# Two attentions: the first unit's loads between the stores, dummy products on PE, and other orders

## The chip, the cores and the metric

The kernel is one program on one core of a Trainium2 chip (trn2). Its time is the device time of the whole program in microseconds, as the median of several runs. PE is the engine of matrix products (TensorE), with PEld for its weight loads; DVE, ACT and POOL are the vector, scalar and general-purpose engines; SP issues transfers. All of them work through their own list of instructions in order and wait for each other by semaphores.

## The reference, cut to what matters

The program is eight layers on 2 x 1024 tokens of width 256. The change touches the first and the seventh, causal attentions with grouped heads: 32 query and 8 key heads of width 8, and 16 query and 4 key heads of width 16. Both are, cut:

```python
q = rope(x @ Wq); k = rope(x @ Wk); v = x @ Wv      # 4 query heads share a key head
att = where(causal, q @ k.T / sqrt(hd), -inf)        # 1024 x 1024 for each head
y = softmax(att) @ v
x = x + y @ Wo + b
```

## The kernel before, in words

`Attention` (one class for both widths, `hd`) works in units: one key head of one batch with its four query heads, 1024 positions. Width 8 has 16 units, width 16 has 8. Positions are cut in blocks of 128.

**Preparation.** For each of four groups of 512 tokens, PE makes the projections, DVE rotates them, PE transposes them, and ACT writes each as three bf16 parts (`part1` to `part3`, L952; PE takes the parts off with `less1` and `less2`, L1039). SP stores the parts to DRAM, twelve stores, n = 0 to 11 (L699), from a ring of five buffers; ACT waits until the buffer of store n - 5 is free. Stores 0 to 5 are the first batch's.

**Loads.** `load_copy` brings a unit's queries and keys back in the layout for the products, six transfers of queries (L667) and three of keys (L668). Width 8 loads each unit twice, to partitions 0 and 64 (`copies`), so that two products can run in both halves of PE; `max_at` is 64 there, and 0 in width 16, which has one copy.

**A unit.** First come the row maxima, in 22 pieces k (`MAX_STEPS`): PE makes scores without them (`max_scores`, L1116), DVE reduces them (L877). POOL splits the maxima into bf16 parts (L778 to L785), PE transposes them (`turn_max`, L1135; the first unit does it in two halves, `turn_first_max`, L1126), DVE copies them out (L895, L886), and SP puts them as three rows under the unit's queries (`load_max`, L685; `load_first_max`, L679). With these rows the 36 score steps (`scores`, L1162) give scores less their maximum; ACT exponentiates (L996), POOL masks the diagonal (L807), and twelve value products (`values`, four heads each, L1178) sum into one bank. ACT copies the sum (L988), PE transposes it (`turn_out`, L1143), DVE normalizes (L907, L910).

**Order.** All engines follow the tables in `ORDERS`. The maxima of a unit stand between the score steps of the unit before it, or of the one before that: `max_at` gives the step for each k, negative ones in the unit two ahead. `turn_max`, `turn_out1`, `turn_out0` give the steps of the transpositions, `values_at` those of the value products, `own_at` (first unit alone) those of its own second half of maxima. Products of maxima and the transpositions go through a ring of two bank pairs: each waits until DVE has emptied the item two before it. A unit's first max_scores (k = 0) waits for its loads:

```python
if k == 0:
    pe.wait_ge(self.q_in1.sem, self.q_in1.at((u + 1) * (16 * len(self.terms))))
...
if self.max_at and k == (HALF1 if u == 0 else 0):
    pe.wait_ge(self.q_in0.sem, self.q_in0.at((u + 1) * (16 * len(self.terms))))
```

`warm` (L127) issues products of 512 columns whose result nobody reads.

## Time and profile before

| | |
|---|---|
| median of 3 runs | 1870.91 us (1862.11 to 1872.44) |
| the profiled execution | 1867.24 us, its span 1865.5 us |
| busy in the span | PE 1723.6, DVE 1125.2, ACT 800.0, POOL 539.3 us |
| width 8: preparation, units | 20 to 59.5 us, 59.5 to 490 us |
| width 16: preparation, units | 1369 to 1412 us, 1412 to 1658 us |

Busy time over the whole span says little, since the layers have different limits; the windows and the waits of a stretch tell which engine the others stand behind. The granted clock is that of PE, as a share of its upper level of 2.4 GHz; 0.50 is its lower level, 1.2 GHz.

### The profile page before, as it was taken

The page shows a single profiled execution, that of the slowest core. Times are in us where ns is not written, and L with a number is a line of the kernel's source. Part 1 is how long each engine was busy: PE and PEld are TensorE (multiplying, and loading weights), DVE is VectorE, ACT ScalarE, POOL GpSimd, SP SyncE. Part 2 cuts the span into 40 slices and gives each one's busy share as a digit, 9 for nine tenths or more (in the row PEclk, how much of TensorE's full clock was granted, in tenths as well). Part 3 has the DMA queues.
Part 4 walks back from the last instruction along what each step waited for, and adds up shares of the span by engine and source line. Part 5 has one row for each costly group of instructions (what it writes and reads, how often), then busy time and mean ns, then how long its engine had stood idle before and what let it go on. Part 6 is the DMA issues. An engine that isn't in the chain of part 4 may idle for free.

```text
span 1865.5 us, 32053 instructions
## 1 busy us (share of the span) xinstructions
PE 1723.6 (92%) x10972; PEld 1038.9 (56%) x10972; DVE 1125.2 (60%) x3171; ACT 800.0 (43%) x1469; POOL 539.3 (29%) x852
## 2 busy tenths in 40 slices
PE   7689999999999999898999989999986999999997
PEld 4122222222579998466999946667552333355774
DVE  6689999998442221875222265834566988836444
ACT  3368888888533331113233211222132677752221
POOL 2412222222211111551121140257324122221770
PEclk9689999999999999989999999999986999999999
DMA  3322222221310000301000050123513222001334
GB/s 113 86 59 69 68 67 66 61 63 45 100 61 24 29 24 25 97 1 57 24 27 27 21 192 8 53 74 102 155 49 79 44 44 41 6 2 59 96 102 147
DMA packets 86045, 115.03 MB, mean 62 GB/s; under 512 B 20186, under 2 KB 63874, under 8 KB 85634
## 3 DMA queue, kind: packets, MB, share of 16 engines
q1 hardware_dynamic: 74753, 82.58, 15.9%
q0 software_dynamic: 11136, 30.42, 5.1%
q8 instruction: 92, 1.51, 0.3%
q14 instruction: 64, 0.52, 0.1%
HBM read 78.30 MB, written 33.69 MB: 60 GB/s over the span
## 4 chain that ended last, share of the span: by engine, by line
PE 64%; DVE 22%; DMA 5%; issue 2%; ACT 1%; POOL 1%; SPq 1%; DVEq 0%; ACTq 0%; POOLq 0%
PE psum L1665 15%; DVE region_a L877 15%; PE psum L1677 7%; PE psum L1178 6%; PE psum L1909 5%; PE psum L1162 5%; PE psum L1116 4%; PE psum L1880 4%; PE psum L1891 2%; DMA y_norm<-region_a 2%; PE psum L1928 2%; PE psum L1929 2%; PE psum L437 2%; PE psum L1018 1%; PE psum L2356 1%
## 5 line engine op out<-in xcount | busy, mean ns | idle before, releaser
L877 DVE CUSTOM_DVE_ANT_0 region_a<-psum,region_a 128x128 bf16<-128x128 f32 (+7 forms) x768 | 533.3, 754 | 64.9 <-PE psum L1116 61.7
L996 ACT ACTIVATE region_w<-psum 128x512 f32<-128x512 f32 x864 | 463.2, 601 | 166.7 <-PE psum L1162 152.2
L1178 PE MATMUL psum<-region_w,region_a 128*32 128x512 f32 (+3 forms) x2304 | 245.3, 504 | 2.4 <-issue 0.6
L1764 DVE TENSOR_TENSOR region_a<-psum,region_a 128x512 f32<-128x512 f32 x76 | 52.5, 691 | 297.3 <-PE psum L1665 297.3
L807 POOL TENSOR_SCALAR_AFFINE_SELECT region_w<-region_w 128x512 f32<-128x512 f32 x192 | 121.9, 635 | 370.7 <-ACT region_w L996 297.5
L1116 PE MATMUL psum<-region_a,y_norm 48*128 48x512 bf16 (+7 forms) x816 | 184.7, 356 | 22.9 <-DVE region_a L877 20.4
L1162 PE MATMUL psum<-y_norm,region_a 51*128 51x512 bf16 (+1 forms) x612 | 180.9, 396 | 12.8 <-DMA y_norm<-region_a 10.7
L1546 POOL DMA_INDIRECT region_a<-token_rows,region_a x116 | 113.6, 980 | 161.8 <-DVE region_a L1522 81.9
L1665 PE MATMUL psum<-region_a,ctx 128*128 128x128 f32 x1280 | 148.0, 277 | 1.1 <-DVE region_a L1739 1.1
L1665 PEld LDWEIGHTS psum<-region_a,ctx 128*128 128x128 f32 x1280 | 147.5, 194 | 2.5 <-DVE region_a L1739 1.6
L1162 PEld LDWEIGHTS psum<-y_norm,region_a 51*128 51x128 bf16 (+1 forms) x612 | 46.5, 96 | 172.1 <-ACT region_w L996 121.7
L1677 PE MATMUL psum<-region_w,region_a 128*128 x608 | 137.7, 380 | 1.4 <-ACT region_a L1701 1.4
L1665 PE MATMUL psum<-region_a,y_norm 128*128 128x128 f32 x1152 | 131.7, 275 | 1.8 <-DVE region_a L1739 1.8
L1665 PEld LDWEIGHTS psum<-region_a,y_norm 128*128 128x128 f32 x1152 | 131.3, 192 | 3.1 <-DVE region_a L1739 2.3
L1550 POOL DMA_INDIRECT answer_rows<-region_a x38 | 37.5, 987 | 322.7 <-ACT region_a L1701 322.7
L1677 PEld LDWEIGHTS psum<-region_w,region_a 128*128 128x128 f32 x608 | 112.6, 190 | 15.9 <-issue 2.2
L1116 PEld LDWEIGHTS psum<-region_a,y_norm 48*128 48x128 bf16 (+1 forms) x816 | 52.2, 98 | 102.4 <-DVE region_a L877 71.9
L1909 PE MATMUL psum<-region_w,region_a 128*128 x312 | 108.1, 470 | 0.5 <-issue 0.4
L1178 PEld LDWEIGHTS psum<-region_w,region_a 128*32 128x32 f32 x2304 | 47.8, 108 | 91.2 <-issue 47.9
L1701 ACT ACTIVATE region_a<-psum 128x256 f32<-128x256 f32 x38 | 14.6, 383 | 182.7 <-PE psum L1677 182.7
L1722 ACT ACTIVATE region_a<-psum 128x512 f32<-128x512 f32 x76 | 44.8, 589 | 103.6 <-PE psum L1665 103.6
L1880 PE MATMUL psum<-y_t,region_w 128*128 128x512 f32 (+1 forms) x192 | 86.1, 596 | 0.9 <-ACT ctx L1995 0.9
(226 smaller groups left out, 2539.1 us busy)
## 6 DMA issues: line engine op xcount, KB each, us to landing
y_norm<-a_q SPq DMA_DIRECT2D x132, 64.0 KB
token_rows<-y_norm SPq DMA_DIRECT2D x16, 512.0 KB, 4.7
y_norm<-answer_rows SPq DMA_DIRECT2D x16, 512.0 KB, 6.1
y_norm<-b_q SPq DMA_DIRECT2D x36, 128.0 KB
region_w<-in_f_wg SPq DMA_DIRECT2D x8, 512.0 KB, 4.4
region_w<-in_f_wu SPq DMA_DIRECT2D x8, 512.0 KB, 4.3
region_w<-in_f_wd SPq DMA_DIRECT2D x1, 4096.0 KB, 14.5
region_w<-answer_rows SPq DMA_DIRECT2D x8, 512.0 KB, 8.5
```

Source lines behind the costliest of these rows:

```text
L807: pool.affine_select(p, p, pattern=[[0, GQ], [1, P]], channel_multiplier=-1, base=0, compare_op=ALU.is_ge, fill=0.0)\
L877: last = dve.tensor_tensor_reduce(self.masked_scores[place % 2][:, at:at + n], both[:, at:at + n], self.causal[:, SEQ - n:SEQ], scale=-1.0 ...
L996: act.activation(self.p[col % P_RING][:, :, i % 4, :], c.bank[ST_BANKS[s % 3]].rearrange("p (h t) -> p h t", h=GQ), ACT.Exp, scale=self.sc ...
L1116: mm = pe.matmul(c.bank[bank + b][:, to:to + cols], qp[rows, h, P * i:P * i + P], kp[rows, lo:lo + cols], start=True, stop=True, skip_grou ...
L1162: mm = pe.matmul(bank[:, :], self.kp[slot][rows, P * j:P * j + P], self.qp[slot][rows, :, P * i:P * i + P], start=True, stop=True)
L1178: mm = pe.matmul(c.bank[ACC_BANK][32 * h:32 * h + 32, P * lo:512], self.vp[slot][:, j, :], self.p[col % P_RING][:, h, lo:4, :], start=(j = ...
L1546: pool.indirect_dma_start(y, None, self.c.tokens[:, :], bass.IndirectOffsetOnAxis(ap=self.row_in[:, k:k + 1], axis=0)).then_inc(done.sem, 16)
L1665: mm = pe.matmul(bank[:, P * q:P * q + P], w[:, f, 512 * half + P * q:512 * half + P * q + P], self.yt[:, f, :], start=(f == 0), stop=(f = ...
L1677: mm = pe.matmul(c.bank[7][:, 0:D], self.h[k % 2][:, j, :], self.wd[:, bass.ds((own * (last + 1) + j) * D, D)], start=(j == 0), stop=(j == ...
L1764: dve.tensor_tensor(h[:, at], c.bank[2 + half][:, :], self.g[:, at], ALU.mult)\
L1880: mm = pe.matmul(c.bank[6 * (n % 2) + k][0:m, :], weight[:, f, P * j:P * j + m], c.yt[:, f, 512 * g:512 * g + 512], start=(f == 0), stop=( ...
L1909: mm = pe.matmul(self.gu_bank[j][:, 0:2 * self.hidden], self.yt[j][:, f, :], w.wgu[:, f, bass.ds(owner[k] * (2 * self.hidden), 2 * self.hi ...
```

## The change

Three things change in both attentions. The nine loads of unit 0's copy are cut into three parts (`load_part`) and stand between stores 6 to 8 (the second copy of width 8 between 9 to 11), where they stood in one piece behind store 5 (and 8); on SP, unit 1's copy at partition 0 moves behind the first half of unit 0's rows. PE gets dummy products: 10 in the last group of the preparation, 33 between unit 0's first ten maxima, two in each of its first six steps. The tables of `ORDERS` get other numbers: both of width 8, and the first unit's of width 16. The diff:

```diff
--- before.py
+++ after.py
@@ -75,17 +75,17 @@
         return [k for k, at in enumerate(self.own_at, len(MAX_STEPS) - len(self.own_at)) if at == s]
 
 
-VALUES_8 = [8, 13, 16, 18, 20, 24, 26, 32, 35, 38, 41, 42]
+VALUES_8 = [6, 9, 19, 19, 21, 23, 28, 30, 33, 36, 38, 39]
 VALUES_16 = [6, 9, 12, 17, 22, 28, 31, 35, 35, 38, 41, 41]
 ORDERS = {
-    8: (FirstOrder([0, 0, 0, 0, 0, 0, 0, 0, 1, 1, 1, 2], 6, 9,
-                   [5, 6, 9, 9, 9, 9, 12, 14, 14, 14, 14, 16, 16, 18, 19, 20, 20, 21, 21, 24, 24, 26],
-                   30, 10, 34, VALUES_8, 6, 17, 28),
-        Order([-11, -10, -9, -4, -4, -1, 1, 2, 3, 5, 6, 8, 8, 9, 11, 13, 14, 17, 18, 20, 21, 22],
-              30, 10, 29, VALUES_8, 6, 17, 24)),
-    16: (FirstOrder([0, 1, 2, 2, 2, 2, 3, 4, 5, 5, 6, 7], 8, 9,
-                    [8, 8, 9, 9, 9, 10, 12, 13, 13, 14, 16, 16, 17, 18, 18, 20, 20, 20, 22, 22, 24, 28],
-                    32, 33, 23, VALUES_16, 5, 19, 28),
+    8: (FirstOrder([1, 2, 2, 2, 2, 2, 2, 2, 2, 3, 3, 3], 5, 9,
+                   [0, 1, 3, 3, 6, 7, 9, 9, 9, 9, 9, 9, 10, 12, 12, 12, 14, 16, 18, 20, 21, 22],
+                   28, 15, 26, VALUES_8, 3, 18, 24),
+        Order([-12, -9, -6, -6, -4, -3, -1, 1, 2, 3, 5, 6, 7, 9, 10, 12, 14, 16, 19, 20, 21, 22],
+              28, 15, 26, VALUES_8, 3, 18, 25)),
+    16: (FirstOrder([0, 1, 2, 2, 3, 3, 3, 4, 4, 5, 5, 6], 7, 9,
+                    [7, 8, 8, 9, 9, 9, 10, 11, 12, 12, 12, 12, 13, 13, 13, 15, 16, 18, 21, 22, 23, 23],
+                    33, 33, 33, VALUES_16, 5, 19, 27),
          Order([-9, -8, -7, -5, -2, -1, 0, 0, 3, 4, 6, 6, 8, 8, 10, 12, 13, 14, 17, 19, 21, 23],
                33, 33, 25, VALUES_16, 5, 19, 29)),
 }
@@ -656,18 +656,20 @@
                          (self.bias_out, d["bias_out"].partition_broadcast(P)),
                          (self.mq, d["mq"])):
             sp.dma_start(dst, src).then_inc(self.wo_in.sem, 16)
+        def load_part(u, slot, at, a):
+
+            q_in, k_in = (self.q_in1, self.k_in1) if at == self.max_at else (self.q_in0, self.k_in0)
+            row = at + hd * sum(1 for term in self.terms if term[0] < a)
+            n = sum(1 for term in self.terms if term[0] == a)
+            q = self.q_dram[a, bass.ds(u * (GQ * hd), GQ * hd), :].rearrange("(h d) t -> d h t", d=hd)
+            for m in range(n):
+                sp.dma_start(self.qp[slot][row + hd * m:row + hd * m + hd, :, :], q).then_inc(q_in.sem, 16)
+            sp.dma_start(self.kp[slot][row:row + hd * n, :], self.k_dram[0:n, bass.ds(u * hd, hd), :])\
+                .then_inc(k_in.sem, 16)
+
         def load_copy(u, slot, at):
-
-            q_in, k_in = (self.q_in1, self.k_in1) if at == self.max_at else (self.q_in0, self.k_in0)
-            row = at
             for a in range(3):
-                n = sum(1 for term in self.terms if term[0] == a)
-                q = self.q_dram[a, bass.ds(u * (GQ * hd), GQ * hd), :].rearrange("(h d) t -> d h t", d=hd)
-                for m in range(n):
-                    sp.dma_start(self.qp[slot][row + hd * m:row + hd * m + hd, :, :], q).then_inc(q_in.sem, 16)
-                sp.dma_start(self.kp[slot][row:row + hd * n, :], self.k_dram[0:n, bass.ds(u * hd, hd), :])\
-                    .then_inc(k_in.sem, 16)
-                row += hd * n
+                load_part(u, slot, at, a)
 
         def load(u, slot):
             for at in reversed(self.copies):
@@ -698,17 +700,19 @@
             sp.wait_ge(self.part3.sem, self.part3.at(n + 1))
             sp.dma_start(dst.rearrange("a f t -> f a t"), self.parts[n % PARTS][0:rows, :, :])\
                 .then_inc(self.parts_out[n % PARTS].sem, 16)
-            if n == 3 * NG // NB - 1:
-                self.parts_stored(sp, n + 1)
+            later = n - 3 * NG // NB
+            if later == 0:
+                self.parts_stored(sp, n)
                 sp.wait_ge(self.pads.sem, self.pads.at(self.slot_pads * 2))
-                load_copy(0, 0, self.max_at)
-            if n == 3 * NG // NB + 2 and self.max_at:
-                load_copy(0, 0, 0)
+            if 0 <= later < 3 * len(self.copies):
+                load_part(0, 0, self.copies[-1 - later // 3], later % 3)
         for q_in, k_in in ((self.q_in0, self.k_in0), (self.q_in1, self.k_in1))[0 if self.max_at else 1:]:
             sp.wait_ge(q_in.sem, q_in.at(16 * len(self.terms)))
             sp.wait_ge(k_in.sem, k_in.at(48))
-        load(1, 1)
+        load_copy(1, 1, self.max_at)
         load_first_max(0)
+        for at in self.copies[:-1]:
+            load_copy(1, 1, at)
         self.parts_stored(sp, 3 * NG)
         sp.wait_ge(self.pads.sem, self.pads.at(self.slot_pads * SLOTS))
 
@@ -1050,6 +1054,11 @@
             for q in range(4):
                 if g < NG:
                     multiply(4 * g + q)
+                elif q == 1:
+                    pe.wait_ge(self.v_done.sem, self.v_done.at(NT))
+                    c.warm(pe, 3, 2)
+                elif q:
+                    c.warm(pe, 3, 3)
                 if g > 1 and q == 0:
                     less2(n - 1)
                 if g and q == 0:
@@ -1064,9 +1073,9 @@
                 if g and q == 3:
                     less1(n + 2)
                     less2(n + 1)
+        c.warm(pe, 3, 2)
         less2(3 * NG - 1)
 
-        pe.wait_ge(self.v_done.sem, self.v_done.at(NT))
         pe.wait_ge(self.rotm.sem, self.rotm.at(3 * NT if hd == 8 else NT + 1))
         pe.wait_ge(self.wo_in.sem, self.wo_in.at(16 * 3))
 
@@ -1195,6 +1204,8 @@
                 if left > 1:
                     for k in self.order.early_maxima(s):
                         max_scores(u + 2, k, (slot + 2) % SLOTS)
+                if first and s < order.values_at[0]:
+                    c.warm(pe, ACC_BANK, 2)
                 if left and s == order.turn_max:
                     turn_max(u + 1)
                 if not first and s == order.turn_out1:
@@ -1209,10 +1220,16 @@
 
         for k in range(HALF1):
             max_scores(0, k, 0)
+            if k == 1:
+                pe.wait_ge(self.part3.sem, self.part3.at(3 * NG))
+            if k:
+                c.warm(pe, ACC_BANK, 2)
+        c.warm(pe, ACC_BANK, 5)
         turn_first_max(0)
         for k in range(HALF1, HALF1 + 4):
             max_scores(0, k, 0)
-        pe.wait_ge(self.part3.sem, self.part3.at(3 * NG))
+            c.warm(pe, ACC_BANK, 3)
+        c.warm(pe, ACC_BANK, 6)
         self.each_unit(unit)
         for col, at in enumerate(self.order.values_at):
             if at >= len(STEPS):
```

The first place is SP's queue behind store 5, at the end of the preparation of width 8 (stores are a_q and a_k as targets, loads have them as sources). Before:

```order
L699 DMA a_k<-region_a 64x3x512
L667 DMA y_norm<-a_q 8x4x1024 x3
L668 DMA region_a<-a_k 24x1x1024
L667 DMA y_norm<-a_q 8x4x1024 x2
L668 DMA region_a<-a_k 16x1x1024
L667 DMA y_norm<-a_q 8x4x1024
L668 DMA region_a<-a_k 8x1024
L699 DMA a_q<-region_a 128x3x512 x2
L699 DMA a_k<-ctx 64x3x512
L667 DMA y_norm<-a_q 8x4x1024 x3
```

With the change:

```order
L701 DMA a_k<-region_a 64x3x512
L701 DMA a_q<-region_a 128x3x512
L666 DMA y_norm<-a_q 8x4x1024 x3
L667 DMA region_a<-a_k 24x1x1024
L701 DMA a_q<-region_a 128x3x512
L666 DMA y_norm<-a_q 8x4x1024 x2
L667 DMA region_a<-a_k 16x1x1024
L701 DMA a_k<-ctx 64x3x512
L666 DMA y_norm<-a_q 8x4x1024
L667 DMA region_a<-a_k 8x1024
L701 DMA a_q<-ctx 128x3x512
L666 DMA y_norm<-a_q 8x4x1024 x3
```

Stores 6, 7 and 8 each stand ahead of a part of the loads, and no longer behind all nine.

The second place is PE at unit 0's first score step of width 8 (the product whose inputs wait for the rows, m_in0), with the semaphores that each waits for. Before:

```order
L1162 MATMUL psum<-y_norm,region_a 128x512 [waits attn_k_in0,attn_m_in0,attn_q_in0,attn_part3]
L1116 MATMUL psum<-region_a,y_norm 128x512 [waits attn_ring_done]
L1116 MATMUL psum<-region_a,y_norm 128x256
L1116 MATMUL psum<-region_a,y_norm 128x512 [waits attn_ring_done]
L1116 MATMUL psum<-region_a,y_norm 128x256
```

With the change:

```order
L127 MATMUL psum<-identb 128x512 x9
L1171 MATMUL psum<-y_norm,region_a 128x512 [waits attn_m_in0,attn_k_in0,attn_q_in0]
L1125 MATMUL psum<-region_a,y_norm 128x128 [waits attn_q_in0,attn_ring_done,attn_k_in0,attn_k_in1,attn_q_in1]
L1125 MATMUL psum<-region_a,y_norm 128x128 x3
L127 MATMUL psum<-identb 128x512 x2
L1171 MATMUL psum<-y_norm,region_a 128x512
L1125 MATMUL psum<-region_a,y_norm 128x512 [waits attn_ring_done]
L1125 MATMUL psum<-region_a,y_norm 128x256
```

Behind the first score product now stands k0 of unit 1 (four products of 128 columns), which waits for both copies of unit 1; before, unit 0's own maxima k10 and k11 stood there.

The third place is PE in a steady unit of width 8 around the transposition of the next unit's maxima (L1135 before, L1144 with the change), from step 27 on. Before:

```order
L1116 MATMUL psum<-region_a,y_norm 128x384 x2
L1162 MATMUL psum<-y_norm,region_a 128x512 x2
L1143 MATMUL psum<-identf,region_a 128x128 x4
L1162 MATMUL psum<-y_norm,region_a 128x512
L1135 MATMUL psum<-identb,region_a 96x128
L1162 MATMUL psum<-y_norm,region_a 128x512 x2
L1116 MATMUL psum<-region_a,y_norm 128x384 x2
L1116 MATMUL psum<-region_a,y_norm 128x512 x2
L1178 MATMUL psum<-region_w,region_a 32x512 x4
L1162 MATMUL psum<-y_norm,region_a 128x512 x3
L1116 MATMUL psum<-region_a,y_norm 128x512 x2
L1178 MATMUL psum<-region_w,region_a 32x512 x4
```

With the change, from step 27 too:

```order
L1171 MATMUL psum<-y_norm,region_a 128x512
L1125 MATMUL psum<-region_a,y_norm 128x256 x4
L1171 MATMUL psum<-y_norm,region_a 128x512
L1144 MATMUL psum<-identb,region_a 96x128
L1187 MATMUL psum<-region_w,region_a 32x512 x4
L1171 MATMUL psum<-y_norm,region_a 128x512 x2
L1125 MATMUL psum<-region_a,y_norm 128x384 x4
L1187 MATMUL psum<-region_w,region_a 32x512 x4
L1171 MATMUL psum<-y_norm,region_a 128x512 x2
L1125 MATMUL psum<-region_a,y_norm 128x512 x2
L1171 MATMUL psum<-y_norm,region_a 128x512
L1125 MATMUL psum<-region_a,y_norm 128x512 x2
```

The transposition moved from behind step 30 to behind step 28, the maxima of 384 columns (k2, k3) from both sides of it to behind it, and a value product stands right behind it.

## Rows read from the trace of the kernel before

**Rows 1.** Windows: width, busy us by engine (instructions), clock, DMA share, GB/s.

```profile
74.30:122.30 48.00, 38.06 (x195) 8.69 (x195) 40.20 (x117) 18.89 (x36) 5.70 (x15) 0.65 0.10 23
197.30:221.60 24.30, 22.58 (x189) 6.27 (x186) 23.20 (x69) 20.08 (x38) 5.97 (x14) 1.00 0.24 65
```

**Rows 2.** Waits of DVE from 148 to 442 us: total, times, longest.

```profile
DVE region_a L877 <- PE psum L1116: 12.8, 24, 1.0
```

**Rows 3.** Timeline of one steady unit, width 8: start, us, engine, instruction.

```profile
213.81 0.29 DVE L877 CUSTOM_DVE_ANT_0 region_a<-psum,region_a 128x128 bf16<-128x128 f32 x1
...
214.28 1.06 PE L1178 MATMUL psum<-region_w,region_a 128*32 128x512 f32 x8
...
215.07 0.24 POOL L785 TENSOR_TENSOR region_a<-region_a 128x32 bf16<-128x32 f32 x1
...
218.00 0.56 DVE L877 CUSTOM_DVE_ANT_0 region_a<-psum,region_a 128x384 bf16<-128x384 f32 x1 [0.30 <-PE psum L1116]
...
222.25 0.82 DVE L877 CUSTOM_DVE_ANT_0 region_a<-psum,region_a 128x640 bf16<-128x640 f32 x1 [0.76 <-PE psum L1116]
```

**Rows 4.** Chain of waits, same unit: start us, us, what.

```profile
217.22 0.24 PE psum L1135
...
217.49 0.23 DVE region_a L895
...
218.52 2.85 DMA y_t<-region_a
```

**Rows 5.** Windows at the clock's fall, width 8.

```profile
55.00:57.00 2.00, 0.00 (x0) 0.00 (x0) 0.00 (x0) 1.05 (x3) 2.00 (x4) 1.00 0.49 161
57.00:59.00 2.00, 1.78 (x4) 0.41 (x4) 0.00 (x0) 1.78 (x5) 2.00 (x4) 0.52 0.39 116
```

**Rows 6.** Timeline, end of the preparation, width 8: ACT, then SP's queue.

```profile
48.16 1.09 ACT L952 ACTIVATE region_a<-psum 128x512 bf16<-128x512 f32 x2 [0.65 <-PE psum L1039]
...
55.95 0.59 ACT L952 ACTIVATE region_a<-psum 64x512 bf16<-64x512 f32 x1 [1.96 <-DMA a_q<-region_a]
...
46.70 1.01 SPq L667 DMA_DIRECT2D y_norm<-a_q  x3
...
57.57 0.33 SPq L668 DMA_DIRECT2D region_a<-a_k  x1
...
61.84 0.99 SPq L667 DMA_DIRECT2D y_norm<-a_q  x3
```

**Rows 7.** Chain of waits, beginning of width 8.

```profile
51.18 4.68 DMA a_q<-region_a
...
59.56 0.55 PE psum L1116 x4
...
71.78 2.41 DMA y_norm<-region_a
...
74.33 0.58 PE psum L1162
```

**Rows 8.** Chain of waits, beginning of width 16.

```profile
1401.75 6.52 DMA b_q<-region_a
...
1411.96 0.55 PE psum L1116 x4
```

**Rows 9.** Windows of width 16.

```profile
1398.00:1406.00 8.00, 4.43 (x22) 2.19 (x20) 2.08 (x7) 3.67 (x7) 6.20 (x9) 0.96 1.02 213
...
1424.00:1450.00 26.00, 22.46 (x91) 6.23 (x89) 22.67 (x64) 9.32 (x15) 3.63 (x9) 0.70 0.17 27
...
1500.00:1525.00 25.00, 24.89 (x172) 9.10 (x170) 21.98 (x62) 19.85 (x37) 5.77 (x13) 1.00 0.17 26
```

**Rows 10.** Timeline of PE at the last unit's turn, width 8.

```profile
465.37 0.59 PE L1162 MATMUL psum<-y_norm,region_a 51*128 51x512 bf16 x3 [1.16 <-DMA y_norm<-region_a]
```

**Rows 11.** Waits of SP's queue from 60 to 62 us.

```profile
SPq L709 <- DMA region_a<-a_k: 0.8, 1, 0.8
```

**Rows 12.** Groups by line: the dummy products elsewhere in the program.

```profile
L127 PE MATMUL psum<-identb 128*128 128x512 bf16 x214 | 52.7, 395 | 0.0
```

## The prediction

> **What bounds the kernel now.** I read the page first, then the chain of waits, and split the two attentions (head width 8 at 20 to 490 us, head width 16 at 1370 to 1658 us) into windows. The rest of the program is not touched. The profiled execution took 1867.24 us, 1865.5 of it span; the median of the three runs shown is 1870.91 us, 3.67 above. The sum below is made against 1867.24.
>
> In width 8 a steady unit takes 24.3 us, and DVE works 23.20 us of it [rows 1]. DVE bounds, and what can be won there is DVE's idle time: 12.8 us in 24 waits from 148 to 442 us, which are twelve units, so 1.07 a unit [rows 2]. It comes at two places. DVE stands 0.30 us behind the copy of the rows (maxima k3 are not yet made), and 0.76 us at the turn of the unit [rows 3]. The second is the rows' own transfer: PE's transposition of the maxima runs at 217.22, although POOL had its parts ready at 215.07 + 0.24 = 215.31 [rows 3, 4]; DVE copies at 217.49, and the transfer lands at 218.52 + 2.85 = 221.37 [rows 4]. Only then does PE start the score product of step 0, with every later maximum queued behind it, and DVE goes on at 222.25 [rows 3].
>
> The beginnings are worse. From 74.3 to 122.3 us DVE works 40.20 of 48.0, and PE has a granted clock of 0.65, which is mostly its 1.2 GHz level [rows 1]. The clock fell behind a stretch (55 to 57 us) in which PE did nothing [rows 5]: ACT waited 1.96 us for store 6 [rows 6], which stood on SP behind nine loads and took 4.68 us to land [rows 7]. In width 16 the same store took 6.52 us [rows 8]. Later width 16 is PE's: 24.89 of 25 us busy [rows 9].
>
> **Steady order of width 8.** The table moves the transposition from step 30 to 28, the normalization of the unit's first half from 29 to 26, and lets seven maxima instead of six of the unit after next stand ahead of step 0. By the rows: the last maximum ends at 213.81, where k0 starts [rows 3]. DVE has from there k0 (0.86), the normalization (0.52) and k1 (1.38; estimates, made of the unit's 23.20 us over its maxima's columns), until 216.57, and copies the rows until 216.8, 0.9 us earlier than 217.72 [rows 4]. PE is at the transposition in time, since only one score product and k1 stand ahead of it. The rows land 3.65 us behind the copy, as now [rows 4], at 220.45. PE gets to step 0 by its own work at about 221.0 (four value products of 1.06 [rows 3] less their overlap, ten score products, five maxima), so the rows are no longer waited for. Late next: the values of column 6 now stand between transposition and k2, so k2 comes at 215.5 + 1.0 + 0.55 = 217.05, 0.26 us after DVE is free, and those of column 9 ahead of k7, some 0.2. Of 1.07 us, 0.61 goes: 12 x 0.61 = **-7.3 us**. Bounds: 0 (the value products take all of it) and -12.8 (all idle time goes [rows 2]). The transfer for the last unit, which PE awaits 1.16 us [rows 10], also starts two steps earlier: **-1.0** (0 to -1.16). The other moves of values and copies in the steady table are set at nothing, since ACT works 20.08 of 24.3 us [rows 1] and waits for them in that gap; what they cost if the gap is used up is a rival. The last unit, alone on PE and ACT: 0, by one either way.
>
> **The beginning of width 8.** Removed: ACT's 1.96 us. Store 6's last part was ready at 48.16 + 1.09 = 49.25 [rows 6] and was issued at 51.15, 0.03 ahead of its transfer [rows 7]; now it goes first. Added on SP between stores: unit 0's nine loads to partitions 64 and up, as three parts of 1.9, 1.6 and 0.85 us (together 4.35; from 46.70 [rows 6] to the store at 51.15 it is 4.45). With two stores between them (0.4 and 0.6) the last is issued at about 55.1. Its price of landing is not shown alone; the nearest row is the last load of unit 0's other copy, issued by 57.9, for which SP waited 0.8 us [rows 11] until 61.75, just ahead of its next load at 61.84 [rows 6]: 3.85 us. So the first maximum's product can start at 58.9 against 59.56 [rows 7], although PE would be ready at 57.0 (59.56 less the 1.96 and some 0.6 that its products there lose to the lower clock): **-0.7**. The ten dummies there cost 0.246 us each (52.7 us / 214 [rows 12]) and lie in PE's waits.
>
> The Trainium skill bears on this length. The Trainium skill (DMA: Bandwidth & Descriptors, "Queues, rings and completion order") says that on each DMA engine the descriptors of a ring are taken in ring order, and a semaphore's increment comes behind that engine's earlier writes. By that, stores issued behind a load do not hold it up, and the load would land in the 2.41 us that a rows transfer takes [rows 7]; the first product would then start at 57.5 and not at 58.9, 1.4 us better. The 3.85 us were measured with three stores right behind the load; no run here separates the two yet.
>
> Then the same time runs through SP again: unit 0's copy at partition 0 goes out between stores 9 to 11 (last load at about 61.9, landing 65.7), SP waits for it, issues unit 1's copy at 64 (4.4) until 70.1 and then unit 0's rows. In the kernel before SP issues all 18 loads of unit 1, from 61.84 [rows 6], ahead of these rows, whose transfer starts at 71.78 [rows 7]. Issue and transfer (0.45 + 2.41) and the step to PE, which starts at 74.33 [rows 7], now end at 73.5: **-0.8** in all.
>
> What is late next is the costliest item that I find. The first unit's table puts maxima k0 of unit 1 at step 0, and max_scores waits there for both copies of unit 1. Copy 0 is now issued behind the rows, 71.0 to 75.6, and lands at 79.5 by the 3.85 us, at 78.0 by 2.4. PE stands at k0 for some 5 us with everything queued behind it, and DVE, which would have gone on at 74.4, does so at 79.4: **+5.0**. An idle PE had the lower clock behind it before [rows 5], so I count on the lower level here again. Against that, DVE has 7.8 us of idle time from 74.3 to 122.3 [rows 1], and the new table puts ten maxima ahead of or right behind the two waits of that stretch; I take 4.2 of the 7.8 as won: **-4.2**. Together the beginning comes out at **0**: at best -0.8 + 3.0 - 7.8 = -5.6 (copy 0 lands early, no idle time left), at worst -0.8 + 5.0 = +4.2 (nothing won behind it).
>
> **The beginning of width 16.** ACT's wait for its store goes [rows 8], but now the loads bind: 960 KB of loads and 960 KB of stores kept the DMA engines full from 1398 to 1406 [rows 9], 8 us. Started behind store 6 (ready at 1398.9) they end at about 1408.2 to 1410, and the first product starts at 1409.7 against 1411.96 [rows 8]: **-2.2**. PE waits some 4 us for that, so the clock falls as it does now. The 33 dummies of the first ten maxima at that level (0.43 each, twice 0.246 less the overlap) take more than DVE's maxima do: I give back **+2.2**. They should raise the clock for PE's 22.46 busy us of 1424 to 1450, which had 0.70 [rows 9]: at the upper level these are 15.7, 6.7 less; 12 dummies at 0.246 take 3.0 of it back, and no more than DVE's idle time there is to be had (26.0 - 22.67 = 3.3 [rows 9]): **-2.0**, kept, as PE bounds what follows. Bounds: -2.2 - 3.3 = -5.5 and +2.2.
>
> **Sum.** -7.3 - 1.0 + 0 - 2.0 = -10.3: 1867.24 - 10.3 = **1856.9**, say 1857 us.
>
> **Rivals.** (1) The beginnings pay too: loads land in 2.4 us, the clock stays up. -7.3 - 1.0 - 5.6 - 5.5 = -19.4, 1848 us. For it: much idle time is there [rows 1, 9]. Against it: PE's wait for unit 1's second copy stands in the order. Chance 0.17.
>
> (2) The wait only moves. If the values of column 6 hold k2 back by their full 1.06 us [rows 3], DVE's idle time in a unit is about what it was, and only the ends change: -1.0 + 0 - 2.0, 1864 us. For it: PE is busy 22.58 of 24.3 us [rows 1], so three value products between steps 28 and 33 may crowd it. Against it: PE's busy time counts products that overlap. Chance 0.27.
>
> (3) Slower: values of columns 2 and 3 both stand at step 19 now. The ring of four value operands holds ACT's exponential of step 18 until column 2 is done, and the copy of the accumulator behind it until column 3 is done. ACT has 24.3 - 20.08 = 4.2 us of slack in a unit [rows 1], some 1.4 of it between steps 1 and 22 by DVE's pace. It decides once the two waits exceed 1.4 us; a unit then grows by up to 0.9 and 14 units by 12.6: 1880 us. I make the wait 0.3 to 0.7. Chance 0.06.
>
> **How the numbers follow.** The forecast has 0.50: 1857, its own range 1850 to 1863. A measurement of this kernel tells about 0.5% from no change, 9.4 us on 1870.91: faster is below 1861.6, slower above 1880.3. Faster: 0.85 of the forecast, all of rival 1, a tenth of rival 2: 0.62. Slower: the upper half of rival 3 and heads that lose in both attentions, 0.05. The same: 0.33. The range leaves out rival 3, the lower third of rival 1 and the top of rival 2: 1846 to 1868.
>
> **What would show it.** Right: landings of the rows 23.8 to 23.9 us apart, no wait of PE on them, one DVE wait of 0.2 to 0.3 behind the copy of the rows; store 6 with no wait on ACT; a PE wait of 3 to 6 us for loads at about 74 us, with the clock at 0.5 behind it. Wrong: landings still 24.4 apart (rival 2), or no PE wait at 74 us and a clock of 1.0 through the first unit (rival 1). A unit with longer ACT waits at step 18 is rival 3. A landing of the loads that is far from 3.85 us moves the beginnings by that difference.

## The result, and the profile after

The changed kernel is slower by 0.7%: 1882.58 us (median of 17, 1867.07 to 1891.47) against 1870.52 (17 runs, 1862.11 to 1874.63), ratio 1.0066 with an interval of 1.0049 to 1.0082. The profiled execution took 1881.02 us, 1879.3 of it span: 13.8 more than before.

The rows below are the three rows of maxima that SP puts under a unit's queries. SP issues those of each next unit when DVE has copied them, so these issues mark the units. Units are numbered from 0, as in the kernel; what the expectations call unit 2's rows in width 8 are unit 1's. In SP's timeline the distances are, in us:

| stage | before | after | change | forecast |
|---|---|---|---|---|
| width 8, first store to unit 1's rows | 87.67 | 97.63 | +10.0 | 0 |
| from there 14 units on, to unit 15's rows | 341.5 | 344.1 | +2.6 | -7.3 |
| last unit, to the router's load of `in_numbers` | 51.13 | 52.59 | +1.5 | -1.0 |
| width 16, first store to unit 6's rows | 223.18 | 228.52 | +5.3 | -2.0 |

The rest of the program, which the change does not touch, took 5.6 us less. A profile varies by that much there: the stretch between the two attentions took 863 to 870 us in the profiles of this study.

**The steady units.** Rows of width 8 after, as SP issues them:

```profile
250.76 1.50 SPq L687 DMA_DIRECT2D y_norm<-region_a  x2
276.10 1.50 SPq L687 DMA_DIRECT2D y_norm<-region_a  x2
302.56 1.50 SPq L687 DMA_DIRECT2D y_t<-region_a  x2
329.09 1.50 SPq L687 DMA_DIRECT2D y_norm<-region_a  x2
353.09 1.50 SPq L687 DMA_DIRECT2D y_norm<-region_a  x2
```

Most distances are 24.0 us (24.47 before), as 329.09 to 353.09 is. But the first three shown are 25.34, 26.46 and 26.53, and further on there is one of 26.71. Windows of the same units (columns as in [rows 1]), and of the last unit:

```profile
226.73:250.76 24.03, 23.08 (x193) 6.81 (x189) 23.37 (x69) 19.76 (x38) 6.12 (x13) 1.00 0.23 66
250.76:276.10 25.34, 24.22 (x193) 7.12 (x189) 23.36 (x69) 19.73 (x38) 6.12 (x13) 0.93 0.24 63
475.00:500.00 25.00, 23.99 (x160) 5.94 (x152) 1.10 (x4) 20.86 (x41) 5.12 (x9) 0.86 0.14 45
```

The same work takes longer where the granted clock is below 1.00, that is, at 1.2 GHz for part of the unit; this is called a fall below. Before, there was none in the steady units, and a shorter one in the last:

```profile
125.00:475.00 350.00, 324.77 (x2693) 91.26 (x2685) 318.17 (x936) 288.74 (x549) 88.82 (x186) 1.00 0.23 62
475.00:500.00 25.00, 22.85 (x149) 12.93 (x149) 6.30 (x21) 14.26 (x28) 4.50 (x8) 0.93 0.46 146
```

The four long distances hold 9.0 us more than four of 24.02; without them the order's gain would be 6.4.

What PE did ahead of the fall at 266.4 us, in its timeline (three of its rows) and ACT's (one), in two windows, and in ACT's waits from 150 to 440 us (total, times, longest):

```profile
260.80 0.85 PE L1187 MATMUL psum<-region_w,region_a 128*32 128x384 f32 x8
264.59 0.63 PE L1152 MATMUL psum<-identf,region_a 128*128 128x128 f32 x4 [0.49 <-DVE region_a L881]
267.10 1.51 PE L1187 MATMUL psum<-region_w,region_a 128*32 128x256 f32 x16
268.30 0.60 ACT L1000 ACTIVATE region_w<-psum 128x512 f32<-128x512 f32 x1 [1.55 <-PE psum L1187]
```

```profile
261.65:266.65 5.00, 4.33 (x25) 1.35 (x24) 4.97 (x11) 4.48 (x9) 0.99 (x3) 0.97 0.25 75
266.00:267.00 1.00, 0.89 (x5) 0.11 (x3) 1.00 (x2) 0.75 (x2) 0.00 (x0) 0.68 0.01 2
```

```profile
ACT region_w L1000 <- PE psum L1187: 11.6, 11, 1.7
```

The value products of column 1 end at 261.65; the next, of columns 2 and 3 together (x16), start at 267.10. In the 5.45 us between there are only score products, maxima and a transposition, at the pace of ACT and DVE; this is called the thin stretch below. The row of waits is the hold that rival 3 named: once a unit, an exponential waits about 1.05 us for values (0.77 in the units without a fall). It was not among ACT's waits before. In this unit the hold, from 266.75 to 268.30, comes behind the fall at 266.4, so the fall is not its work.

**The beginning of width 8**, in the chain of waits from 55 to 131 us (its shares by line, then pieces):

```profile
by line: DVE region_a L881 25.2%; PE psum L1125 15.5%; PE psum L127 15.1%; PE psum L1187 11.8%; PE psum L1171 11.1%; DMA region_a<-a_k 9.6%; SPq L666 4.1%; issue 2.3%; SPq L667 1.8%; SPq L681 1.0%; SPq L701 0.8%; PE psum L1152 0.8%; PE psum
...
56.23 4.01 DMA region_a<-a_k
60.25 0.14 issue
60.39 0.82 PE psum L1125 x8
...
68.20 3.10 PE psum L127 x7
71.30 0.54 PE psum L1135 x4
...
78.69 3.27 DMA region_a<-a_k
81.95 0.14 issue
82.09 0.40 PE psum L1125 x4
```

ACT's wait for store 6 is gone. The last load lands 4.01 us behind the start of its issue and 3.50 behind its end, from which the 3.85 assumed was counted. But dummies (L127) make up 15.1% of the chain, 11.5 us, most of them at 0.97 us for two, twice the 0.246 us each of [rows 12]. First product (60.39) to transposition (71.30, L1135) takes 10.9 us, and took 9.0 before, from 59.56 [rows 7] to this row of the same chain:

```profile
68.53 0.59 PE psum L1126 x4
```

PE's wait for unit 1's second copy is the one that was forecast, 4.36 us up to 82.09. The clock around it:

```profile
72.00:82.00 10.00, 5.73 (x26) 1.81 (x25) 3.52 (x9) 0.60 (x1) 0.64 (x1) 1.00 0.26 68
82.00:92.00 10.00, 7.89 (x30) 1.71 (x30) 8.69 (x29) 1.19 (x2) 0.00 (x0) 0.50 0.00 0
```

The dummies do raise the clock (it is 0.50 from 70 to 80 us in the kernels without them, which come below), but for ten microseconds in nearly half of which PE waits; when there is work again, it has fallen. Added up from windows of 5 us, width 8's beginning has some 51 us at the lower level in both kernels.

**The beginning of width 16**: first the chain, then windows. All of it stands 10.06 us later than before, so the first window answers to 1424 to 1450 in [rows 9].

```profile
1415.44 6.09 DMA region_a<-b_k
1421.53 0.14 issue
1421.66 1.44 PE psum L1125 x8
```

```profile
1434.06:1460.06 26.00, 22.01 (x105) 7.54 (x103) 22.63 (x65) 8.50 (x14) 3.57 (x9) 0.89 0.18 30
1460.06:1485.06 25.00, 23.82 (x110) 7.74 (x108) 19.52 (x58) 12.54 (x24) 2.31 (x7) 0.71 0.04 9
```

Here too the clock came up earlier (0.89 for 0.70) and fell again: 0.71 in the second window, where the kernel before had 1.00 (1450 to 1475). By the windows that is some 20 us at the lower level behind the rise.

### The profile page after: what moved, and what is told of

Same layout as the page of the kernel before. It is cut to its first block, busy times and chain, and to the rows that moved or that the text cites. A ratio compares the mean times of both kernels' runs of the same rounds, so it can differ in the third digit from the quotient of the medians.

```text
span 1879.3 us, 32271 instructions
## 1 busy us (share of the span) xinstructions
PE 1760.0 (94%) x11082; PEld 1051.5 (56%) x11082; DVE 1129.7 (60%) x3171; ACT 795.5 (42%) x1469; POOL 538.7 (29%) x852
## 4 chain that ended last, share of the span: by engine, by line
PE 73%; DVE 15%; DMA 3%; issue 2%; POOL 2%; ACT 1%; SPq 1%; DVEq 0%; ACTq 0%; POOLq 0%
PE psum L1682 15%; PE psum L1187 10%; PE psum L1171 8%; DVE region_a L881 7%; PE psum L1694 7%; PE psum L1125 6%; PE psum L1926 4%; PE psum L1897 4%; PE psum L1908 2%; PE psum L1945 2%; PE psum L1946 2%; PE psum L1022 1%; PE psum L1152 1%; PE psum L2373 1%; DVE ln_stats L318 1%
## 5 line engine op out<-in xcount | busy, mean ns | idle before, releaser
L881 DVE CUSTOM_DVE_ANT_0 region_a<-psum,region_a 128x1024 bf16<-128x1024 f32 (+7 forms) x768 | 537.2, 754 | 80.6 <-PE psum L1125 76.1
L1187 PE MATMUL psum<-region_w,region_a 128*32 128x512 f32 (+3 forms) x2304 | 250.0, 519 | 1.4 <-POOL region_w L811 0.6
L1125 PE MATMUL psum<-region_a,y_norm 48*128 48x512 bf16 (+7 forms) x816 | 186.6, 358 | 25.1 <-DVE region_a L881 12.6
L1171 PE MATMUL psum<-y_norm,region_a 51*128 51x512 bf16 (+1 forms) x612 | 195.6, 403 | 4.0 <-ACT region_w L1000 0.6
L127 PE MATMUL psum<-identb 128*128 128x512 bf16 x324 | 89.5, 413 | 0.0
```

The costliest lines, as they stand in the source:

```text
L127: pe.matmul(self.bank[bank][:, :], self.identb[:, :], over(self.identb[:, :], 1, 4), start=True, stop=True)
L881: last = dve.tensor_tensor_reduce(self.masked_scores[place % 2][:, at:at + n], both[:, at:at + n], self.causal[:, SEQ - n:SEQ], scale=-1.0 ...
L1125: mm = pe.matmul(c.bank[bank + b][:, to:to + cols], qp[rows, h, P * i:P * i + P], kp[rows, lo:lo + cols], start=True, stop=True, skip_grou ...
L1171: mm = pe.matmul(bank[:, :], self.kp[slot][rows, P * j:P * j + P], self.qp[slot][rows, :, P * i:P * i + P], start=True, stop=True)
L1187: mm = pe.matmul(c.bank[ACC_BANK][32 * h:32 * h + 32, P * lo:512], self.vp[slot][:, j, :], self.p[col % P_RING][:, h, lo:4, :], start=(j = ...
```

## The experiments

The theory formed from this: the steady order wins its half microsecond a unit, and bunched values make the clock fall; the dummies lie on the path of the beginning. Each ratio is to the kernel before as run beside it, whose median was 1868.2 to 1868.9 (1870.5 beside the changed kernel). Each profile is one execution, and the executions of one kernel differ, those of the changed kernel by 24 us.

**The steady order alone, in the kernel before** (the new `Order` and its values; the first unit keeps the old ones).

```diff
+STEADY_8 = [6, 9, 19, 19, 21, 23, 28, 30, 33, 36, 38, 39]
-        Order([-11, -10, -9, -4, -4, ...], 30, 10, 29, VALUES_8, 6, 17, 24)),
+        Order([-12, -9, -6, -6, -4, ...], 28, 15, 26, STEADY_8, 3, 18, 25)),
```

> The kernel before with one part of the change alone: the steady order of width 8, its value steps with it; the first unit keeps its old order, and loads and dummies are as before. Theory (the steady order wins, and the clock takes it back): the rows of a unit are issued 24.00 us apart instead of 24.49, 6.4 us less over the attention, PE no longer waits for rows, but in 2 to 4 of the steady units the granted clock falls to the lower level for 3 to 7 us, at 1.3 to 2.7 us each; the time is 1866 to 1870 us, within 0.3% of before. Rival A (the falls in the steady units are left behind by the slower beginning, not made by the order): the clock stays at 1.00 from 125 to 480 us and the time is 1864 us. Rival B (the new order is slower by itself): the spacing in units without a fall is over 24.49 us.

1887.13 us, ratio 1.0080 (1.0054 to 1.0105): as slow as the whole change or slower, which the intervals do not tell. The profile caught the slowest of six executions. In it the rows are 24.0 apart where the clock holds, but eight of the fourteen distances are 25.3 to 29.5:

```profile
150.00:175.00 25.00, 24.03 (x185) 6.94 (x177) 22.68 (x70) 19.47 (x38) 6.14 (x13) 0.87 0.22 64
```

Both rivals fall; of the theory the mechanism holds, but it takes back far more than it expected. The falls need neither dummies nor late loads.

**The values spread, in the changed kernel.**

```diff
-VALUES_8 = [6, 9, 19, 19, 21, 23, 28, 30, 33, 36, 38, 39]
+VALUES_8 = [6, 9, 13, 18, 21, 23, 28, 30, 33, 36, 38, 39]
```

> The changed kernel with two numbers altered: the values of columns 2 and 3 in width 8 at steps 13 and 18 instead of both at 19. Theory (between the values of step 9 and those of step 19 PE has only score products that wait for ACT and DVE; the clock falls in the steady units there): the clock stays at 1.00 from 130 to 470 us, and the 9.0 us of the four falls are gone from the profile; the median is 6 to 9 us under the changed kernel, 1874 to 1877 us, and its executions lie closer together. Rival A (the falls come with PE's load of 24.1 in 25 us, wherever the values stand): falls as often as now, 1882 us. Rival B (ACT's exponential of step 18, held until column 2 is done, costs time in every unit): the spacing of units without a fall becomes shorter than 24.00 us too.

1867.76 us, ratio to before 0.9990 (0.9978 to 1.0003): 14.8 under the changed kernel by the medians, 13.2 when each is set against the kernel before beside it, by two numbers. No distance is over 24.16. One steady unit, the stretch that answers to 261.65 to 266.65 above, the last unit, and DVE's waits from 150 to 440 us (12.6 us in 29 with the values at 19):

```profile
225.48:249.42 23.94, 22.71 (x193) 6.70 (x189) 23.40 (x69) 19.66 (x38) 6.15 (x13) 1.00 0.23 66
262.60:267.60 5.00, 3.98 (x32) 1.43 (x34) 4.96 (x11) 4.53 (x10) 0.00 (x0) 1.00 0.06 18
475.00:500.00 25.00, 22.35 (x159) 10.56 (x159) 5.26 (x17) 16.91 (x33) 4.28 (x8) 1.00 0.32 104
```

```profile
DVE region_a L881 <- PE psum L1125: 5.2, 20, 0.3
```

The spacing without a fall hardly changes, 23.94 for 24.00, so ACT's hold by itself is worth little in this order (rival B). Rival A, a busy PE, is answered two kernels further on, where PE is busier still and nothing falls. Busy time does not mark the stretch either: PE is busy 4.33 of 5 us ahead of the fall and 3.98 of 5 here, with more products (32 for 25 in the trace). The last unit became 2.9 us shorter too, which the expectation had left out.

The same order alone in the kernel before:

> The kernel before with the new steady order of width 8 alone, its values of columns 2 and 3 at steps 13 and 18. Theory: no falls, rows 23.94 us apart, the beginning as before (87.7 us): 7 to 8 us under before, 1861 to 1863 us. Rival (the beginning of the changed kernel is needed for the steady clock, since the same order alone had nine falls): falls remain, 1875 us or more.

1864.81 us, ratio 0.9993 (0.9980 to 1.0006), 22.3 under the same edit with bunched values. The distances are 23.9 to 24.1 but for the first (25.82), so the rival falls. The beginning took 90.8 us and not 87.7, with the clock below 1.00 up to 125 us, and the time is 2 us above what was expected.

**Dummies in the thin stretch**, the values left at 19:

```diff
+            if self.max_at and u > 1 and 14 <= k <= 17:
+                c.warm(pe, bank, 1)
```

> The changed kernel, its values left at step 19, with four dummy products more in each steady unit: one ahead of each of the maxima k14 to k17, which stand between steps 10 and 16, into the bank that the maximum's product then overwrites. Theory (the clock falls because PE does little between the values of step 9 and those of step 19): 0.9 us of products that nobody reads, in that place, end most falls, and the time is 1869 to 1876 us although PE does more. Rival (what hurts is ACT's exponential of step 18, held until the values of step 19 are done, and not the thin stretch): the falls stay and PE has more to do: 1884 us or more.

1877.95 us, ratio to before 1.0038 (1.0018 to 1.0059). The falls are gone, by four products a unit that nobody reads:

```profile
150.00:275.00 125.00, 123.03 (x984) 36.20 (x984) 119.20 (x360) 101.17 (x194) 31.76 (x69) 1.00 0.25 64
```

```profile
250.55 1.50 SPq L687 DMA_DIRECT2D y_norm<-region_a  x2
275.09 1.50 SPq L687 DMA_DIRECT2D y_norm<-region_a  x2
```

The hold at step 18 became shorter (0.5 us) but remained, and the falls did not. Since the fall also came ahead of the hold in the trace above, it is the thin stretch. PE is busy 24.6 of 25 us here at a clock of 1.00. Whether the same dummies elsewhere in the unit would do as well was not tried. The time expected was too low, since the dummies widen every unit to 24.54.

**The old steady order with bunched values.**

```diff
+STEADY_8 = [8, 10, 19, 19, 20, 24, 26, 32, 35, 38, 41, 42]
-              30, 10, 29, VALUES_8, 6, 17, 24)),
+              30, 10, 29, STEADY_8, 6, 18, 24)),
```

> The kernel before with the values of columns 1 to 3 of its steady units moved from steps 13, 16 and 18 to 10, 19 and 19, the copy of the accumulator one step later, and nothing else. Theory (bunched values make the clock fall): falls appear in the old order too, at several of the units between 125 and 440 us, and the time is 1878 to 1890 us. Rival (the falls belong to the new table's other numbers or to its closer spacing): the clock stays at 1.00 from 122 to 440 us, 1868 to 1873 us.

1901.26 us, ratio 1.0186 (1.0170 to 1.0203), more than expected. Falls appear in about half of the units, and those without one are 25.9 us apart instead of 24.47:

```profile
225.00:250.00 25.00, 22.91 (x180) 6.13 (x179) 21.37 (x60) 18.34 (x36) 5.35 (x12) 0.93 0.23 64
250.00:275.00 25.00, 22.27 (x185) 6.54 (x181) 22.37 (x62) 19.22 (x38) 5.54 (x11) 1.00 0.26 64
```

```profile
ACT region_w L997 <- PE psum L1179: 13.7, 11, 1.6
```

Bunching makes the clock fall in the old order too. Its direct cost, some 1.4 us a unit, is larger than the falls' 1.1 each. Here ACT's waits for values are 1.2 us each, little longer than in the changed kernel, so why they cost more is open.

**Without the dummies**, first in the changed kernel (all its `c.warm` lines out), then with the values spread as well.

> The changed kernel without its dummy products; the waits stay where they were put. Theory (the dummies lie on the path while PE has its lower clock, and do not keep it at the upper one): unit 0's transposition stands some 3 us nearer to its first product (10.9 us now, about 9 before), the first half of the maxima of width 16 takes 12.8 us again instead of 15.1, the first six steps lose 2 dummies each at 0.48 us a piece; together 5 to 9 us faster than the changed kernel, 1874 to 1878 us. Rival: without them the lower clock lasts longer in the first units (over 55 us in width 8, where it is 51 in both kernels now), and the time is 1883 us or more.

> The changed kernel with the values of columns 2 and 3 at steps 13 and 18, and without the dummy products. Theory (two separate losses, in the steady units the bunched values, in the beginnings the dummies): from the first store to the rows of unit 2 it takes 89.5 us as without dummies (97.6 with them), the fourteen units behind it 335.1 us at a clock of 1.00; width 8 is then 6 us shorter than before, the time 1860 to 1864 us. Rival (the dummies of the beginning are what keeps the clock up later): falls in the steady units as without dummies alone, 1870 us or more.

1878.07 us (1.0056, 1.0041 to 1.0072), and 1860.59 us (0.9960, 0.9945 to 0.9975). The two losses are separate, as expected, and without both the change is 0.4% faster than before. Width 8's beginning takes 89.5 and 91.8 us instead of 97.6 and 97.7, though it has the lower clock nearly throughout. The chain of the second kernel, whose transposition comes 9.0 us behind the first product again:

```profile
60.27 0.60 PE psum L1121 x4
...
69.29 0.59 PE psum L1131 x4
...
77.45 4.13 DMA region_a<-a_k
```

**Which dummies.** Three kernels with spread values keep some: those of the preparation alone, those of width 8 alone, those of width 16 alone.

> The changed kernel with the values at 13 and 18 and only the ten dummies of the preparation; those of the first ten maxima and of the first six steps are left out. Theory (a dummy costs where PE is waited for: behind the landing of the loads, not ahead of it): the ten lie in PE's wait for the loads and cost nothing, the beginning of width 8 takes 90 to 92 us as without any, and the time is 1859 to 1862 us. Rival (the dummies of the preparation cost too, because they delay the products of the last parts): half of the 7 us that all the dummies cost stays, 1864 us.

> The changed kernel with the values at 13 and 18, its dummy products kept in width 8 alone. Theory (in width 8 the dummies lie on the path while PE has its lower clock): the beginning of width 8 takes 96 to 98 us (91.8 without), that of width 16 85 to 86 us to unit 1's rows, and the time is 1864 to 1867 us. Rival (the loss of 7 us is width 16's, where the clock fell a second time with dummies): 1860 to 1862 us.

> The changed kernel with the values at 13 and 18, its dummy products kept in width 16 alone. Theory (in width 16 they cost too, because the clock that they raise falls again at about 30 us behind unit 0's first score step): unit 1's rows are issued 91 to 93 us behind the first store instead of 85.4, with a second stretch at the lower clock, and the time is 1863 to 1866 us. Rival (that second fall is chance and not the dummies'): 85 to 88 us, and 1860 to 1861 us.

1860.13 (0.9954, 0.9937 to 0.9972), 1865.84 (0.9988, 0.9971 to 1.0006) and 1860.40 us (0.9960, 0.9940 to 0.9980). In the preparation, where PE waits for the loads, dummies cost nothing. Those of width 8 cost 5.3 us by the medians, and its beginning is 97.75 us. Those of width 16 show no cost, against the theory: by the medians -0.2 us here and 1.9 beside the dummies of width 8 (1867.76 for 1865.84), which the intervals do not tell from nothing. Width 16's unit 1 had its rows 86.4 us behind the first store, and the clock rose early and fell only briefly:

```profile
1425.00:1450.00 25.00, 20.52 (x97) 6.12 (x95) 23.03 (x66) 6.70 (x12) 2.93 (x8) 0.86 0.25 40
1450.00:1475.00 25.00, 24.42 (x169) 8.36 (x169) 22.07 (x66) 17.47 (x33) 5.54 (x12) 1.00 0.25 42
```

So the +5.3 in the table above is not shown to be a cost of the dummies. The distance to unit 1's rows came out between 85 and 94 us in the profiles of the study, with one and the same code for width 16 at 86.5 and 92.8, by where the clock fell. Still, three of the five profiles with all of width 16's dummies have it at 92 and none of the six without any does, so a cost of a microsecond or two is not excluded.

**The wait for unit 1's second copy**: all 18 loads ahead of unit 0's rows, as before, in the changed kernel and in the one with spread values and no dummies; and, in the latter, the old order of the first unit.

```diff
-        load_copy(1, 1, self.max_at)
+        load(1, 1)
         load_first_max(0)
-        for at in self.copies[:-1]:
-            load_copy(1, 1, at)
```

> The changed kernel with SP's order of before at one place: all 18 loads of unit 1 stand ahead of unit 0's rows. Theory (the wait for unit 1's second copy, 4.36 us at 82.09 us in the changed kernel, costs its length): the rows are issued 4.8 us later, at about 77.1 us, and land at 79.5; the first score product starts there, k0 of unit 1 right behind it, and DVE goes on at about 81 instead of 84.2 us; 3 us faster, 1879 us. Rival (what counts is when unit 0's rows land, and the stretch behind is bound by PE at its lower clock): no difference, 1882 us, or slower.

> The changed kernel with the values at 13 and 18, without dummies, and with all 18 loads of unit 1 ahead of unit 0's rows, as before. Theory (PE's wait for unit 1's second copy costs its length also at the lower clock): the same edit took 3.2 us off the beginning of width 8 in the kernel with dummies (97.6 to 94.4 us); here 91.8 becomes 88 to 89 us and the time 1857 to 1859 us. Rival (without dummies DVE bounds that stretch and the later rows cost what the wait gave): 1860 to 1863 us.

> The changed kernel with the values at 13 and 18, without dummies, and with the first unit's order of width 8 as before, which puts k0 of unit 1 at step 5 and has no wait there for unit 1's second copy. Theory: the wait is taken out of PE's way, 91.8 us of the beginning become 88 to 89, the time 1857 to 1859 us. Rival (the first unit's new table saves as much behind the wait as the wait costs, as the prediction had it): no difference, 1860 to 1862 us.

1882.53 us (1.0069, 1.0053 to 1.0085), 1858.81 (0.9942, 0.9929 to 0.9956) and 1860.16 (0.9956, 0.9942 to 0.9970). The loads' old place shortens the beginning by 3.2 us (97.63 to 94.39) and by 2.1 (91.75 to 89.61). In the first kernel falls hide it, since nine of the fourteen distances in its profile are above 25 us; in the second it is 1.8 us by the medians, less than the two intervals can tell apart. There PE waits for the rows at step 0, and finds unit 1's copies landed:

```profile
79.27 0.58 PE L1165 MATMUL psum<-y_norm,region_a 51*128 51x512 bf16 x1 [6.26 <-DMA y_norm<-region_a]
```

The first unit's old table makes no difference (91.83 us): what it saves at the wait it loses behind it. The kernel of 1858.81 us is the fastest found, 0.6% under before.

**No store behind the loads** of unit 0's first copy, with spread values and no dummies.

```diff
+            if self.max_at and n == 9:
+                sp.wait_ge(self.q_in1.sem, self.q_in1.at(16 * len(self.terms)))
+                sp.wait_ge(self.k_in1.sem, self.k_in1.at(48))
```

> The changed kernel with the values at 13 and 18, without dummies; in width 8 stores 9 to 11 and what follows them on SP wait until unit 0's first copy has landed, so that no store is issued behind these loads. The last load then shows its landing without stores behind it: 3.91 us in the kernel with them. Theory 1 (stores behind a load hold it up): about 3.3 us, as the last load of unit 1's second copy, which has nothing behind it (3.27 us). Theory 2 (what is issued behind a load does not delay it): 3.9 us again. The rest of the beginning gets longer by the later loads.

One run, 1865.48 us. The last load and what SP issues next:

```profile
56.65 0.50 SPq L667 DMA_DIRECT2D region_a<-a_k  x1
60.56 0.39 SPq L704 DMA_DIRECT2D a_q<-ctx  x1
```

The chain has 3.77 us for its landing, against 3.67 to 4.01 with stores issued right behind. That is theory 2, in one run; theory 1's 3.27 us of unit 1's copy was no measure of it, since the same load, with nothing behind, took 2.8 to 4.1 us in nine profiles.

Another place in the traces speaks against theory 2 as a general rule. In the changed order nine loads are issued right behind the rows of unit 0. In the kernel with spread values and no dummies, whose rows were issued by 72.62, PE then got to step 0 at:

```profile
76.90 0.58 PE L1167 MATMUL psum<-y_norm,region_a 51*128 51x512 bf16 x1 [4.20 <-DMA y_norm<-a_q]
```

That is 4.28 us behind the issue. In six kernels with these loads behind the rows and no dummies ahead of step 0 it is 1.5 to 4.3 us, over 2.3 in five of them; in the six kernels that issue nothing there it is 1.8 to 2.2. This suggests that what follows a small load can hold it up; no run here was made to show it.

## Why the prediction was wrong, step by step

- **Steady order, main term (-7.3).** The mechanism was right. PE's waits for the rows are gone (before: 7.9 us in 11 waits from 150 to 440), and the spacing without a fall is 24.0, forecast 23.8 to 23.9: 6.4 us over the fourteen distances. That this is near 7.3 is partly luck. The sum multiplied 0.61 us by the twelve units of its window, not by fourteen, which would give 8.5; a unit won 0.46.
- **The step that failed first**: "The other moves of values and copies in the steady table are set at nothing, since ACT works 20.08 of 24.3 us". Rival 3 looked at the right place, step 19, but priced only ACT's hold, which costs 0.06 us a unit (24.00 for 23.94). What the move costs is the clock: it falls in the stretch without values from step 9 to 19, which took 9.0 us in the profile and 2.9 in the last unit; spreading them gave back 13 to 15 by the medians. So the time is near rival 3's 1880 by chance. The profile of before had shown no fall in a steady unit, and no term of the sum and no rival allowed for one.
- **The step that failed second**: in width 8 the sum counted the ten dummies of the preparation and left out the 33 and 12 of the first unit, at 0.49 us each at the lower clock, on PE, for which DVE waits. That is 5.3 us by the medians, 5.9 in the profiles (97.63 for 91.75). For width 16 they were priced (2.2 us, measured 2.3 between first product and step 0: 15.1 us for 12.8).
- **First product, width 8 (-0.7)**: about -0.1 by the first store. The last load's issue ended 23.7 us behind the first store (23.0 forecast) and landed 3.50 us later (3.85 forecast).
- **Unit 0's rows (-0.8)**: without dummies they were issued 0.8 us earlier by the first store, as forecast (38.08 for 38.88), but step 0 started 1.7 us later (43.90 for 42.25): from issue to product it took 2.5 us more, with nine loads behind the rows.
- **Wait for unit 1's copy (+5.0 - 4.2)**: the wait was there, up to 82.09 (79.4 forecast), and the old first order, which has none, is no faster, so these two terms cancel as forecast. The whole beginning did not come out at 0: without dummies it is 4.1 us longer than before (91.75 for 87.67). Undoing the loads' move wins 2.1 of them. The other 2 are not taken apart; the two kernels with the steady order alone, whose beginning has the old loads and the old first order, took 90.8 and 91.6 as well.
- **Landing rule.** The prediction took the rows' 2.41 us for what follows if stores issued behind a load do not hold it up; its sum did not use this. The loads take 3.8 without such stores. The Trainium skill (DMA: Bandwidth & Descriptors, "Queues, rings and completion order") says that on each DMA engine the descriptors of a ring are taken in ring order. The 3.77 us against 3.67 to 4.01 fit with that, but the rows above suggest that this order alone does not keep a load from being delayed by what follows.
- **Last unit (-1.0)**: PE's wait of 1.16 us [rows 10] is gone, but nearly nothing was won. The last unit before had a fall of its own (the 0.93 above); four profiles with spread values and a like fall have 50.96 to 51.10 us for 51.13. The 49.73 us of five others are those without a fall.
- **Width 16 (-2.0)**: the loads took 6.09 us to land, and the first product came 0.4 us earlier by the first store, not 2.2. No gain and no cost of the dummies is shown. Without them unit 6's rows come 222.2 to 224.9 us behind the first store (six profiles; 223.18 before): nothing that these profiles can tell was won. The +5.3 of the one profile goes with where the clock fell.

With the two failed steps taken out, the change measures 1860.59, 7.9 us under before as run beside it; the forecast of all of it was 1857. How the 7.9 divides is not shown: in the profiles of the two kernels the four stages of the table together are 3.7 us shorter (+4.1, -6.8, -0.2 and -0.8), and the rest lies in the stretches that the change does not touch.

Open: why the clock falls in one steady unit and not in the next, which has the same stretch. How many fall differs as well: four, four, eight and nine long distances in the profiles of four kernels with this steady order and bunched values.

## What to carry to other kernels

When an order is changed, look at how evenly it spreads PE's products, not only at what each engine waits for: here a stretch with fewer products, though PE was never idle for long in it, cost the clock for part of the unit. Dummy products cost nothing here where PE itself waits, and cost time at the lower clock's price where another engine waits for PE; the clock that they raised was worth nothing where PE had to wait again before its work. Two losses in one change can hide a gain: here a change that is worth 8 us without them measured 12 us slower.

## What was not expected of the hardware

The clock fell to 0.50 with PE never waiting longer than 0.49 us in the unit ahead, and four more products of 512 columns a unit, which made the unit 0.5 us longer, kept it at 1.00 throughout. The Trainium skill (TensorE: Matmul & The Clock Gate, "A second HAM failure mode: psum-queue depth-cycling") tells of a kernel in which PE idles briefly but often between groups of products, and its clock swings between the two levels. The traces here agree that the clock can swing without a long wait. They do not show the brief idling as the cause: PE idled more in the same stretch with spread values (3.98 of 5 us busy for 4.33), and the clock held. What decides it here is the place of a few value products: none of the twelve windows of 25 us from 150 to 450 us had a clock below 1.00 with spread values, and eleven had with bunched ones and the same steady order alone.
